# One GNN layer's edge counts: 1300 chunks instead of 1200 on the dense path, dealt to the slots by other weights

## The reference, cut to what matters

```python
dst = minimum((12500 * uniform(400000) ** 2).astype(int32), 199999)   # then src, dst sorted by dst
edge_index = stack([src, dst])
# layer 0
head, tail = x[edge_index[0]], x[edge_index[1]]
att = sigmoid(concatenate([head, relation_emb[edge_type]]) @ att_w + att_b)
aggr = segment_sum(att * tail, edge_index[0], 12500)      # summed by SRC, features read by DST
x = layernorm(x + tanh(aggr @ W_w.T + W_b))
# layers 1 to 3: segment sums by DST of x[src] (plain, then weighted), each with residual and layernorm
```

## Time and profile before

| | us |
|---|---|
| median of three executions | 10662.61 (10654.64 to 10670.87) |
| the profiled execution: device time | 10667.16 |
| its span, first to last instruction | 10665.4 |
| first and last scatter of layer 0 (L730) in it | 106.0 and 3775.8 |
| PE / DVE / ACT / POOL busy over the span | 77% / 75% / 55% / 75% |
| mean granted clock of TensorE | 0.843 |

### The profile page before, as it was taken

One profiled execution on the slowest core, in us unless ns is written; L12 is line 12 of the kernel. 1 busy time (PEld: TensorE's weight loads), 2 busy tenths in 40 slices (PEclk: granted clock), 3 DMA queues, 4 the chain that ended last, 5 costly groups with the idle time before them and its releaser, 6 DMA issues. The chain is left out here.

```text
span 10665.4 us, 146984 instructions
## 1 busy us (share of the span) xinstructions
PE 8239.5 (77%) x41161; PEld 5534.8 (52%) x41162; DVE 7953.8 (75%) x19923; ACT 5860.8 (55%) x13187; POOL 8009.1 (75%) x7169
## 2 busy tenths in 40 slices
PE   3887888888888745666666689888888799888887
PEld 2444444444444433555555556655556556555556
DVE  7777777777777657665555499988887699888776
ACT  3766555555555435444433278755554587655553
POOL 4788778888888857777777667777777677777775
PEclk7877777777777757777788789999999899999998
DMA  6433333343333341111111111111111111111111
GB/s 157 48 36 37 36 35 39 38 39 38 39 39 39 38 96 29 29 29 28 29 28 28 29 33 29 30 29 29 29 28 27 38 29 29 29 29 29 27 28 33
DMA packets 651809, 397.35 MB, mean 37 GB/s; under 512 B 456994, under 2 KB 563748, under 8 KB 649745
## 3 DMA queue, kind: packets, MB, share of 16 engines
q0 software_dynamic: 445920, 252.47, 19.4%
q1 hardware_dynamic: 201276, 132.08, 4.9%
q10 hardware_dynamic: 3814, 3.37, 0.2%
HBM read 283.23 MB, written 104.16 MB: 36 GB/s over the span
## 5 line engine op out<-in xcount | busy, mean ns | idle before, releaser
L809 POOL DMA_INDIRECT mem<-xt,mem x5175 | 4900.5, 947 | 1651.2 <-issue 1567.3
L730 POOL DMA_INDIRECT table<-mem,idx x1925 | 2998.3, 1558 | 748.6 <-issue 560.9
L1156 PE MATMUL ps<-mem 128*128 128x392 f32 (+5 forms) x6750 | 2609.3, 502 | 157.4 <-DVE mem L1723 70.8
L951 ACT ACTIVATE mem<-iota_f,mem 128x128 f32<-128x128 f32 x4200 | 1319.5, 390 | 2051.8 <-PE ps L1156 1943.3
L1723 DVE TENSOR_TENSOR mem<-mem,ps 128x392 f32 (+3 forms) x3300 | 1915.9, 581 | 461.0 <-PE ps L1156 422.4
L1706 DVE TENSOR_SCALAR mem<-ps,mem 128x392 f32<-128x392 int16 (+5 forms) x4050 | 2173.3, 556 | 0.0
L1196 PE MATMUL ps<-mem 128*65 128x64 f32 (+2 forms) x7590 | 1010.9, 273 | 1349.9 <-DMA mem<-xt,mem 1348.5
L1196 PEld LDWEIGHTS ps<-mem 128*65 128x65 f32 (+2 forms) x7590 | 816.4, 174 | 1884.2 <-DMA mem<-xt,mem 1751.7
L1156 PEld LDWEIGHTS ps<-mem 128*128 128x128 f32 (+1 forms) x6750 | 1112.1, 178 | 745.8 <-issue 352.2
L930 ACT COPY mem<-zero_c 128x564 f32<-128x564 f32 x1260 | 894.9, 732 | 670.0 <-PE ps L1174 341.8
L1014 PE MATMUL ps<-mem 128*128 128x392 bf16 (+2 forms) x2400 | 789.2, 462 | 500.5 <-DVE mem L1467 394.1
(11 more groups left out here) (186 smaller groups left out, 9445.3 us busy)
## 6 DMA issues: line engine op xcount, KB each, us to landing
mem<-xt,mem POOLq DMA_INDIRECT x5175, 2.4
mem<-key_rows SPq DMA_DIRECT2D x385, 160.0 KB, 3.3
table<-mem,idx POOLq DMA_INDIRECT x1925, 3.2
table<-mem POOLq DMA_DIRECT2D x3, 6304.0 KB, 61.4
mem<-table SPq DMA_DIRECT2D x42, 448.0 KB, 5.2
xt<-xs SPq DMA_DIRECT2D x9, 896.0 KB
mem<-in_x_dram SPq DMA_DIRECT2D x415, 16.0 KB, 2.1
w_d<-mem SPq DMA_DIRECT2D x2, 1562.5 KB, 7.7
```

Source lines behind the costliest of these rows:

```text
L730: pool.indirect_dma_start(out=tables[i % NTAB][:, :], out_offset=bass.IndirectOffsetOnAxis(ap=idx[:, i % (IDXS * GC):i % (IDXS * GC) + 1], ...
L809: pool.indirect_dma_start(out=gbuf[:, o:o + F], out_offset=None, in_=xt[l][:, :], in_offset=bass.IndirectOffsetOnAxis(ap=src_q[q % 2].bitc ...
L951: ins = act.activation(lo_d[:, k * P:(k + 1) * P], iota_f[:, 0:P], ACT.Abs, bias=nslo_q[q % 2][:, c + k:c + k + 1])
L1156: last = pe.matmul(ps_d[b % PSD][:, 0:w], lo_l[:, r * P:(r + 1) * P], blk_l[:, r * DT:r * DT + w], start=(k == 0), stop=(k == parts - 1))
```

## The change

Three things are changed. C0 becomes 1300: 100 chunks move from the scatter path to the dense path, so the loop has 365 slots instead of 385. In the tables of layer 0 a flush group weighs 1.3 instead of 2.4. And in `block_add0` the wait on the previous addition (`d0_add`) is no longer an instruction of its own ahead of the wait for PE; it is carried by the addition.

```diff
-C0 = 1200
+C0 = 1300
 G00 = C0 // GC
 NT0 = NG - G00
@@
 BLOCK0_END, ZONE0_END = slots(SEG_OF0, [0.13 * k * d + 0.24 * d for (_, k), d in zip(BLOCKS[:NB0], ROWS_OF)],
-                              2.4, NU, NT0, 8)
+                              1.3, NU, NT0, 8)
@@
-                if b:
-                    v.wait_ge(d0_add, b)
                 v.wait_ge(blk0_sum, b + 1)
                 new = ps_pair[b % 2].rearrange("p (t c) -> p t c", t=2)[:, :, 0:rows * T]
-                v.tensor_tensor(at, at, new.rearrange("p t (s d) -> p t s d", s=T), ALU.add).then_inc(d0_add, 1)
+                ins = v.tensor_tensor(at, at, new.rearrange("p t (s d) -> p t s d", s=T), ALU.add)
+                if b:
+                    ins._wait_ge(d0_add, b)
+                ins.then_inc(d0_add, 1)
```

## The result

The changed kernel takes 10835.5 us (median of 4 runs, 10833.1 to 10836.4); the kernel before, run beside it, takes 10663.3 us (4 runs, 10654.6 to 10670.9). The ratio is 1.0166, with a 95% interval of 1.0153 to 1.0179: 172 us slower. The forecast was 231 us slower, 10894 us.

What follows compares the result with a forecast made beforehand. The layer-0 loop was taken as bound by the PE, ACT, DVE chain, nearly level with POOL before; slots -52, blocks +141, segments +160, extras +44 us made it 3742 us, the loop 231.5 us longer: 10894 us, range 10785 to 10965.

Steps and rivals of the forecast that it cites:

- Rival 1: Layer-0 loop: POOL stays the bound, so 100 scatters fewer make it faster, 10390 to 10480 us; chance 5%.
- 88 us of stalls: Layer-0 loop, in the POOL-bound rival: up to 88 us of POOL stalls saved if evener dealing removes them.
- Slots, groups, openings: Layer-0 chain: each slot 2.58 us, each flush group 1.28, the first slot of a flush 1.53 more.
- price list: Layer-0 loop: least-squares prices for slots, flush groups, openings, blocks and extras, summing to a chain of 3742 us after.
- 35 x 1.43: Layer-0 slots with both flush groups and blocks: 35 after the change, each 1.43 us extra.
- the extras: Layer-0 chain: surcharges for flush openings, mixed slots and slots with blocks alone, 215 us after the change, +44 us.
- the second fit: Layer-0 chain: prices fitted without slots that follow a wait for a landing (236 left), 3694 us instead of 3742.
- The bounds of 90: Layer-0 additions: the moved wait taken as 0, with 1000 x 0.09 = 90 us to either side as bounds.
- Rival 2: Layer-0 additions: the moved wait frees DVE by 50 to 90 us, 10804 to 10844 us; chance 10%.
- The other weights: Dealing of layer-0 work to slots: evening out wins nothing with nearly all slots above POOL's pace, taken as 0.
- 193 x 0.54: Layer-0 slots with blocks alone: 193 after the change, each 0.54 us extra.
- rivals 3 and 4: Flushes: 3, TensorE's higher clock removes opening costs, 61 us less, 8%; 4, groups cost 2.1 us, +200 us, 4%.

Runs made afterwards that it cites:

- kernels 1 and 3: 1: changed kernel without each slot's fifth scatter, 10806.1 us; 3: kernel before cut into 39 segments instead of 35, 10722.4 us.
- kernel 6: Changed kernel with the wait on the previous addition put back as an instruction of its own ahead of the wait for PE: 10868.5 us, ratio 1.0188.
- kernel 2: Kernel before without the fifth scatter of every slot: 10546.2 us, ratio 0.9897.
- kernel 9: Changed kernel with no block dealt to a slot that has flush groups, on a third chip: 11950.1 us, ratio 1.0155 to the kernel before there.
- kernel 10: Kernel before's 1200 chunks and 35 segments with the moved wait and new weights for groups and blocks, on the third chip: 11711.9 us, ratio 0.9955.

## Why the prediction was right, and where its size was off

- *The bound.* Right. The chain's average decides, not POOL's busy time. Rival 1 was wrong, by kernels 1 and 3, and would have been right at 1100 chunks. (Its "88 us of stalls" stand in no row; the earlier trace rows leave 154.5 - 75.6 = 79 us.)
- *Slots, groups, openings.* Right. I summed the changed kernel's 350 slots by class, measured and by the price list: 40 openings 643.6 us (prices 638.0), 82 further flush slots 881.4 (890.0).
- *Blocks.* The 193 slots with blocks alone took 1810.8 us (prices 1810.7). That they agree so well is luck. With the old wait, in kernel 6, the same slots took 1835.7: they were priced 25 us too low, and the moved wait gave 25 back.
- *Mixed slots.* Wrong. This is the term that was mis-sized most: "35 x 1.43" in the extras. The 35 mixed slots took 347.3 us and not 403.8. A part of these 56.5 us comes back in the block slots: by my price list some 20 of their 25 us stand in the 35 slots right behind the mixed ones. With all classes together the chain of kernel 6 lies 43 us below the forecast. The price was wrong in the kernel before already, by the way the slots for the fit were picked. The fit left out every slot whose copy waited for a landing. Of the 24 mixed slots 9 were left out, and these were the cheap ones, since a message that is ready early waits for POOL. In kernel 2, where POOL holds nothing up, the 15 that were kept take 10.6 us on average and the 9 others 7.9. Nine of the 15 have one group and four to six blocks, and one, slot 43, took 16.2 us. Slots of three groups, as the change deals them, were only among those left out. One is slot 352 with three groups and two blocks. Its message copy and the one before it, in the kernel before (9.31 us) and in kernel 2 (7.39 us):

```profile
3454.62 0.43 ACT L884 COPY mem<-ps 128x320 f32<-128x320 f32 x1 [3.48 <-DMA table<-mem,idx]
3463.93 0.43 ACT L884 COPY mem<-ps 128x320 f32<-128x320 f32 x1 [5.71 <-DMA table<-mem,idx]
```

```profile
3369.32 0.43 ACT L886 COPY mem<-ps 128x320 f32<-128x320 f32 x1 [1.95 <-PE ps L1065]
3376.71 0.43 ACT L886 COPY mem<-ps 128x320 f32<-128x320 f32 x1 [3.70 <-PE ps L1065]
```

  The changed kernel has slots with the same content, and they take 7.39 us too. All engines in one of them (slot 297, lines of some engines left out):

```profile
3247.36 0.43 ACT L884 COPY mem<-ps 128x320 f32<-128x320 f32 x1 [1.95 <-PE ps L1063]
...
3252.47 0.99 PE L1014 MATMUL ps<-mem 128*128 128x490 bf16 x4 [0.71 <-DVE acc L1483]
...
3253.26 1.18 DVE L1465 TENSOR_TENSOR mem<-mem,ps 128x980 f32 x1 [0.93 <-PE ps L1014]
...
3253.39 1.33 PE L1063 MATMUL ps<-mem 64*128 64x64 f32 x10
...
3254.74 1.17 DVE L1465 TENSOR_TENSOR mem<-mem,ps 128x980 f32 x1
3254.76 0.43 ACT L884 COPY mem<-ps 128x320 f32<-128x320 f32 x1 [3.71 <-PE ps L1063]
```

  PE passes both blocks at once (0.99 us), since both PSUM pairs are free after a flush, and goes on to the message's matmuls while DVE still adds. The copy starts at 3254.76, beside the second addition, so the slot takes 7.4 us. A part of the work is only put off: the next slot, with five blocks, took 12.3 us. An extra of 0 would have given 10894 - 50 = 10844 us, and kernel 9, which has no mixed slots, bears that sum out. The prediction had a sign of this: the second fit, without the slots behind a wait for a landing, gave 3694 us. That is 5 us from kernel 6 (3699) and 11 from the changed kernel, and it served only for the range.
- *The moved wait.* Taken as 0; it is 17 to 30 us. The bounds of 90 held it. Rival 2 (50 to 90) named the right sign and two to five times the size. I read the additions whose wait was hidden and missed the one in eight with new offsets. The Trainium skill's figure of 50-100 ns (Advanced Engine Details and Errata, Network/Comms) fits no addition here: the median changed by 0, the one in eight by 120 to 220 ns. Kernel 6 has the chain at 3698.7 us, 43 below the forecast, and the wait took 16 more of it: together the 59 us.
- *The other weights.* Taken as 0; they cost 14 us in the changed kernel. The total didn't miss them: the 193 slots of "193 x 0.54" were counted with the new weights, so the cost already stood among the extras, and the zero was wrong only as a statement of its own.
- *TensorE's clock, rivals 3 and 4.* The openings cost as forecast (16.1 us on average; those with ten groups 17.2, where 17.8 was forecast) and the groups 1.30 us, with a granted clock of 0.75 in the loop in both kernels.
- *What was to be seen.* L884 ends 430 us more of POOL's idle time (forecast "about 420"), but all the idle before L730 grew by 1082.6 - 748.6 = 334 us only. The message copies in a flush, the copies L856 and a three-row addition (0.28 us after its one-hot) came as forecast; the last scatter came at 3948 us and not near 4007. "Almost never waits for a landing" was too strong: 37 times, 171 us.

## What to carry to other kernels

When two paths through a pipeline are nearly level, the busiest engine says little: price a slot on each path and sum both, since the loop takes about the larger. Moving work to another method pays only what the fixed cost of its larger pieces leaves: here, by the price list, 20 slots fewer (52 us of chain) came with five segments (160 us) and 100 blocks (141 us) more. When a price list is fitted to slots, ask which slots the fit leaves out: leaving out those that wait for the other path leaves out the cheap ones.

## What was not expected of the hardware

- A wait carried by the instruction saved 0.12 to 0.22 us where its offsets had just been loaded into registers, and nothing in the median elsewhere.
- Two chips differ by 10% on the same kernel (10663 and 11767 us). The profiles put this into the part behind the loop: kernel 9 takes 3849 us for its scatters there and the changed kernel 3841. The window behind the loop in kernel 10, on the slower chip:

```profile
3705.00:11704.00 7999.00, 5782.15 (x27675) 4141.08 (x27675) 5164.88 (x11610) 3718.79 (x9205) 5018.35 (x5226) 0.82 0.14 28
```

  It takes 7999 us where the earlier trace rows have 6889, with the same counts. DVE, ACT and POOL are as busy as there; PE is 510 us busier at a granted clock of 0.82 instead of 0.89, and the gathers' idle time differs:

```profile
L809 POOL DMA_INDIRECT mem<-xt,mem x5175 | 4912.6, 949 | 2745.5 <-issue 1403.5
```

  It is 2745.5 us on the slower chip and 1648.9 us in the changed kernel's profile. Of the time on the slower chip 991 us end by something that the profile can't name; such waits before L809 are absent in the changed kernel's profile. Why that chip is slower there, and not in the loop of layer 0, stays open.
